# A two-layer scan kernel: the first layer's sums, gates and closings in a new order and in own PSUM banks, and backward steps of the second layer moved by a round

## The reference, cut to what matters

```python
# layer 0, per image, T = 3136 tokens, C = 192
k, v, r = xs @ Wk.T, xs @ Wv.T, xs @ Wr.T
x_bi = 0.5 * (wkv_scan(k, v) + flip(wkv_scan(flip(k), flip(v))))
h    = sigmoid(r) * x_bi
h    = layernorm(h) * ln_g + ln_b
x    = x + h @ Wo.T
# layer 1, per image: two selective scans (16 states, 384 inner channels)
x1, x2 = _layernorm(tok, g1, b1), _layernorm(tok, g2, b2)
x, z = x1 @ W_in_x.T, x2 @ W_in_z.T
y_f  = _branch(x, ...)              # conv of 4 taps, silu, dt, B, C, scan
y_b  = flip(_branch(flip(x), ...))
out  = ((y_f + y_b) * silu(z)) @ W_out.T + b_out
```

## Time and profile before

| | us |
|---|---|
| median of 3 runs | 21059.9 (21033.74 to 21079.35) |
| the profiled execution | 21187.9 |
| its span, first to last instruction | 21186.1 |
| TensorE / VectorE / GpSimd / ScalarE busy | 87% / 83% / 84% / 66% |
| mean granted TensorE clock | 0.912 of 2.4 GHz |

### The profile page before, as it was taken

The page is one execution under the profiler, slowest core; times in us unless marked ns, Lnnn a source line. Parts: engine busy times, 40 slices in busy tenths (PEclk is TensorE's granted clock), DMA queues, the critical chain, the costliest instruction groups (busy, mean ns, idle before and its releaser), DMA issues. The chain is left out here.

```text
span 21186.1 us, 179805 instructions
## 1 busy us (share of the span) xinstructions
PE 18392.8 (87%) x43392; PEld 7798.8 (37%) x43392; DVE 17639.1 (83%) x13967; ACT 14035.8 (66%) x35077; POOL 17697.7 (84%) x10548
## 2 busy tenths in 40 slices
PE   8888888888888888888888888888888888888888
PEld 3333433334333333333333333333333333333333
DVE  7878978889788897878978888787987879878788
ACT  5756757567576775757757577675766757667576
POOL 6978969789697896978969799796987969879699
PEclk8989989899899998989989999998998989989899
DMA  2313313233132331313313133231331313313133
GB/s 74 133 63 123 130 58 132 70 123 129 57 130 74 123 130 67 132 61 123 130 65 133 64 130 121 75 131 66 129 113 72 132 64 132 113 72 128 61 137 115
DMA packets 528855, 2178.88 MB, mean 103 GB/s; under 512 B 96328, under 2 KB 243424, under 8 KB 527648
## 3 DMA queue, kind: packets, MB, share of 16 engines
q1 hardware_dynamic: 527648, 2165.99, 28.3%
HBM read 1905.47 MB, written 245.63 MB: 102 GB/s over the span
## 5 line engine op out<-in xcount | busy, mean ns | idle before, releaser
L969 DVE TENSOR_TENSOR_SCAN arena<-ps,arena 128x897 f32<-128x897 f32 x5376 | 10979.3, 2063 | 762.7 <-ACT arena L1125 688.2
L1177 POOL TENSOR_TENSOR arena<-arena 128x896 f32<-128x896 f32 x5376 | 9985.8, 1873 | 904.4 <-DVE arena L969 560.9
L899 PE MATMUL ps<-arena,ident 128*128 128x448 f32 x21504 | 9168.2, 563 | 1134.1 <-POOL arena L1177 1128.8
L1109 ACT ACTIVATE ps<-arena,A 128x448 f32<-128x448 f32 x10752 | 6403.8, 630 | 2089.7 <-DVE arena L969 2055.6
L899 PEld LDWEIGHTS ps<-arena,ident 128*128 128x128 f32 x21504 | 4070.1, 196 | 5966.4 <-issue 3525.2
L1169 POOL TENSOR_TENSOR arena<-arena 128x896 f32<-128x896 f32 x2240 | 4675.3, 2087 | 0.0
L958 DVE TENSOR_TENSOR arena<-ps,arena 128x896 f32<-128x896 f32 x3136 | 3336.3, 1064 | 30.4 <-ACT ps L1071 30.4
L856 PE MATMUL ps<-arena,diag 128*128 128x448 f32 x5376 | 2181.3, 550 | 117.4 <-issue 115.6
L856 PEld LDWEIGHTS ps<-arena,diag 128*128 128x128 f32 x5376 | 1021.8, 192 | 1185.5 <-issue 1093.8
L1158 POOL TENSOR_TENSOR arena<-arena 128x448 f32<-128x448 f32 x672 | 763.2, 1137 | 455.3 <-DVE arena L938 455.3
L1125 ACT ACTIVATE arena<-arena 128x2 f32<-128x2 f32 x5376 | 1033.1, 192 | 53.3 <-DVE arena L969 53.3
(11 more groups left out here) (164 smaller groups left out, 20641.1 us busy)
## 6 DMA issues: line engine op xcount, KB each, us to landing
arena<-bc_rows SPq DMA_DIRECT2D x1792, 896.0 KB, 4.8
x_projected<-arena SPq DMA_DIRECT2D x112, 672.0 KB, 3.5
y_forward<-arena SPq DMA_DIRECT2D x112, 672.0 KB, 3.7
arena<-x_projected SPq DMA_DIRECT2D x112, 672.0 KB, 7.6
arena<-y_forward SPq DMA_DIRECT2D x112, 672.0 KB, 4.1
x<-in_x SPq DMA_DIRECT2D x119, 336.0 KB, 3.7
x_normed<-arena SPq DMA_DIRECT2D x112, 336.0 KB, 2.8
arena<-x_normed SPq DMA_DIRECT2D x112, 336.0 KB, 4.3
```

Source lines behind the costliest of these rows:

```text
L899: m = e.matmul(y, ident[:, :], pr[:, q % NPR, a * T:a * T + T], start=False, stop=p == NP - 1 and a == 1)
L969: e.tensor_tensor_scan(rev(hh[:, q % NH, 0:W2], s), rev(decays(q)[:, 0:W2], s), rev(bb[:, q % NB, 0:W2], s), car[:, k, n:n + 1] if i % NC ...
L1109: e.activation(two(decays(q))[:, a, :], dt[:, r % NDT, :], ACT.Exp, scale=Am[s][:, k, 2 * p + a:2 * p + a + 1]).then_inc(c_ex, 1)
L1177: e.tensor_tensor(pr[:, q % NPR, :].rearrange("p (a b) -> p a b", a=2), two(hh[:, q % NH, :]), cr[:, 2 * p:2 * p + 2, :], ALU.mult).then_i ...
```

## The change

Two lists of due rounds are changed, and with the first also who does what and in which bank.

First layer:
- The direction sum and the gate are issued tile by tile, an addition and its multiplication together (`HPOOL` and `HDVE`), on GpSimd over rounds 13.6 to 24.6. The tiles t = 0 and t = 1 of the last step (s = 6) go to VectorE (4 operations).
- GpSimd makes `ys` of unit U-3 in round U instead of U-4, behind `tn` instead of ahead of it.
- `BANKS` gives each closing two banks, one for k = 0 (and the sums) and one for k = 1. They are banks that the products, the keys and the recurrences have left by then.
- `mn` is split into `mA` (over the first 128 channels) and `mM` (the other 64). Two closings of one step are issued together: both `mA`, both `mM`, both first halves of `vr`, and so on.
- `rounds` gives every step of the closings its round. Closing 0 starts at 14.4 instead of 17.0, closings 1 and 2 at 18.6 instead of 20, 3 and 4 at 21.2 instead of 23, 5 and 6 at 23.5 instead of 26.

Second layer, all of it but one number on the backward side: `ye` one round later, the gate of tile 0 one round later, all `z1` to `z4` and `g` 0.3 to 0.4 rounds later, `p1` and the step sizes of tiles 0 and 1 by 0.6 to 0.7 rounds, the first convolution by 0.3. The forward side's `p1` goes from 0.9 to 1.2, in the same whole round.

```diff
-    def project(i, t, u):
+    def project(i, t, u, v):
         pe.append((t, "xp", i, 0))
-        act.append((t + 0.9, "p1", i, 0))
+        act.append((t + v, "p1", i, 0))
         sp.append((t + 1.5, "cw", i, 0))
...
-        act.extend([(t + 1.6, "z1", i, e), (t + 2.4, "z2", i, e), (t + 3, "z3", i, e), (t + 3.7, "z4", i, e)])
-        pool.append((t + 4.5, "g", i, e))
+        act.extend([(t + 2, "z1", i, e), (t + 2.7, "z2", i, e), (t + 3.3, "z3", i, e), (t + 4, "z4", i, e)])
+        pool.append((t + 4.8, "g", i, e))
...
-            for e, v in enumerate((1, 8.7, 10.7)):
+            for e, v in enumerate((1.3, 8.7, 10.7)):
                 conv(i, e, t + v)
-            project(i, t + 15.6, (1.2, 1.7, 5))
-            gate(i, 0, t + 20.6)
+            project(i, t + 15.6, (1.9, 2.3, 5), 1.5)
+            gate(i, 0, t + 21.6)
             gate(i, 1, t + 24)
...
-                dve.append((t + 0.5, "ye", i, e))
+                dve.append((t + 1.5, "ye", i, e))
...
+    BANKS = {MID: (JB, JB), MID + 1: (JB, (2, 3)), MID + 2: ((KB, VB), (2, 3)), MID + 3: ((0, 1), JB)}
+
+    def bank(n, k):
+        return ps[:, BANKS[CLOSE[n][0]][k][n % 2], 0:T]
+
+
+    HPOOL = [(MID, 0), (MID, 2), (MID + 1, 0), (MID + 1, 1), (MID + 1, 2), (MID + 2, 0), (MID + 2, 1), (MID + 2, 2),
+             (MID + 3, 2)]
+    HDVE = [(MID + 3, 0), (MID + 3, 1)]
+
...
+    def both_ways(s, t):
+
+        c = NC - 1 - s
+        n = 0 if s == MID else 2 + 3 * (s - MID - 1)
+        if t == 0:
+            return ys[:, 3 * s, :], rev(ys[:, 3 * c + 1, :], 1), n, 3 * s + 1 + (s == MID)
+        if t == 1:
+            return ys[:, 3 * c, :], rev(ys[:, 3 * s + 1, :], 1), n + 1, 3 * s + 2
+        return ys[:, 3 * s + 2, :], rev(sw[:, c, :], 1), n + (1 if s == MID else 2), 3 * s + 3
...
+        for s, t in HPOOL:
+            pool.append((3 * s + 3.6 + (t or s == MID) + (t == 2) * (s > MID), "h", s, t))
+        for s, t in HDVE:
+            dve.append((23.2 + 0.01 * t, "h", s, t))
+        rounds = {
...
+            MID + 2: dict(mA=21.2, mM=21.3, hc=23.3, sq=23.4, vr=23.8, rs=24.3, hn=24.2, o0=24.4, o1=24.6, x0=24.4, x1=24.6),
...
+            if n % 2 or not n:
+                pe += [(r["mA"], "mA", n, 0), (r["mM"], "mM", n, 0), (r["vr"], "vr", n, 0), (r["o0"], "o", n, 0),
+                       (r["o1"], "o", n, 1)]
+            dve += [(r["hc"], "hc", n, 0), (r["hn"], "hn", n, 0), (r["x0"], "xo", n, 0), (r["x1"], "xo", n, 1)]
+            act += [(r["sq"], "sq", n, 0), (r["rs"], "rs", n, 0)]
...
+                if name == "h":
+                    i = HDVE.index((n, k))
+                    a, b, m, units = both_ways(n, k)
+                    w.wait_ge(b_y, units)
+                    w.wait_ge(b_rg, m + 1)
+                    e.tensor_tensor(a, a, b, ALU.add).then_inc(b_hx, 1)
+                    w.wait_ge(b_hx, i + 1)
+                    e.tensor_tensor(a, a, sg[:, m, :], ALU.mult).then_inc(b_hv, 1)
+                    continue
...
+                if name == "mA":
                     w.wait_ge(b_rg, len(GATES))
-                    w.wait_ge(b_h, 3 * (s - MID) + 3)
-                    if n > 1:
-                        w.wait_ge(b_xo, nth(n - 2, 1) + 1)
-                    e.matmul(o, ones[:, :], ha, start=True, stop=False)
-                    e.matmul(o, ones[rows, :], hm, start=False, stop=True).then_inc(b_mn, 1)
+                    if s < MID + 3:
+                        w.wait_ge(b_h, HPOOL.index((s, 1 if s > MID else 0)) + 1)
+                    if s == MID + 1:
+                        w.wait_ge(b_xo, nth(0, 1) + 1)
+                    if s == MID + 2:
+                        w.wait_ge(b_kv, NU)
+                        w.wait_ge(b_bv, NU)
+                    if s == MID + 3:
+                        w.wait_ge(b_hv, len(HDVE))
+                        w.wait_ge(b_dn, NU)
+                    for m in two:
+                        e.matmul(bank(m, 0), ones[:, :], ys[:, 3 * CLOSE[m][1], :], start=True, stop=False)
+                if name == "mM":
+                    gated(w, s)
+                    for m in two:
+                        rows, f = late(m)
+                        e.matmul(bank(m, 0), ones[rows, :], rev(ys[rows, 3 * s + 2, :], f), start=False,
+                                 stop=True).then_inc(b_mn, 1)
...
+                        if k and s == MID + 1:
+                            w.wait_ge(b_dn, NU - 1)
+                        elif k:
+                            w.wait_ge(b_xo, nth(*{MID: (0, 0), MID + 2: (m - 2, 1), MID + 3: (m - 4, 0)}[s]) + 1)
...
-            u = U - 4
-            if 0 <= u < NU:
-                w.wait_ge(b_nw, u + 1)
-                e.tensor_tensor(ys[:, u, :], dn[:, u % 3, T:2 * T], tn[:, u % 2, :], ALU.mult).then_inc(b_y, 1)
+            u = U - 3
+            if 0 <= u < NU:
+                w.wait_ge(b_nw, u + 1)
+                e.tensor_tensor(ys[:, u, :], dn[:, u % 3, T:2 * T], tn[:, u % 2, :], ALU.mult).then_inc(b_y, 1)
```

88 lines of the change are left out of this document (42 added, 46 removed).

## The result

The changed kernel takes **20562.1 us** (20554.2 to 20586.7, 4 runs) against 21069.0 us (21033.7 to 21079.4) for the kernel before: a ratio of **0.976, 95% interval 0.975 to 0.978**, 507 us less. The direction was right and the time lies in the range of 20,400 to 20,960, but 158 us under the 20,720 that I named. The parts show why: one came out as worked out, one brought four times its term, one cost eight times what it was to bring.

The account below looks back on a forecast made before the run. GpSimd, fullest engine, was taken to limit the second layer, with waits around `ye`, and TensorE the first layer's tail. Gains 240 + 112 + 16 = 368 us; 21,060 - 368 + 28 = 20,720 us, range 20,400 to 20,960.

Parts of the forecast that it names:

- Part 1: Second layer, `ye` and backward steps a round later: VectorE scans during its wait, -15 us an item, -240 us in all.
- (b): Second layer, backward side: GpSimd comes to its floor, -4.7 us a chunk, run at 20,470 us; chance 0.12.
- (c): Second layer gains nothing, as TensorE or ScalarE becomes what the scan waits for: 20,960 us; chance 0.15.
- (d): Second layer slower, TensorE's next tile waiting for the later `ye`: +286 us, run at 21,250 or 21,380 us; chance 0.06.
- I give them no sum of their own: Second layer: moves other than `ye` only let the scan follow at once, with no separate gain counted.
- Part 2: First layer's tail behind the last recurrence: fewer matmuls left there, -7 us an item as the mean, -112 us.
- the gap of 4 us: First layer's tail at the upper clock: TensorE waits 4 us ahead of `mM` of closings 5 and 6.
- (e): First layer's tail: banks and pairs do nothing, TensorE being busy anyway; counted in the sum already, no chance given.
- a tail once low stays low: First layer's tail: once at the lower TensorE clock it remains there; used against the 20,400 us rival.
- (a): First layer's tail: clock stays up in nearly all items, 435 us gained instead of 112, run at 20,400; chance 0.14.
- Part 3: First layer, rounds 14 to 20 ahead of the last recurrence's end: about -1 us an item, -16 us.
- the term -4.0: First layer, rounds 14 to 20: VectorE's 4.0 us wait for the edge copy behind GpSimd's block of six goes.

Follow-up runs that it names:

- -17.3 alone: The kernel before with only the second layer's part of the change: 20908.4 us, ratio 0.987; its second layer is 17.3 us an item shorter.
- all alternated: The changed kernel with each closing's 128-partition and 64-partition matmuls issued one behind the other again, not paired: 21168.4 us, ratio to before 1.003.

## Why the prediction was right, and where not

**Part 1** held in mechanism and size. -15 us an item were said and -17.6 measured (-17.3 alone); five backward chunks 367 us, measured 365.78; the wait at `ye` below 300 us, measured 148.5; GpSimd at 355, measured 355.47. The idle time of five backward chunks came down to that of the forward side (10.3 against 12.7 us), which was the row I took the size from. Rivals (b), (c) and (d) fall: GpSimd kept 10.3 of its 23.4 us of idle time, now for TensorE, and TensorE waits at the skip matmul 7.9 us in five chunks (3.6 before), 0.5 at each of 15 places. Wrong in it was "I give them no sum of their own": the other moves are worth 3.0 us on top of `ye`.

**Part 2** was mis-sized: -7 us an item said, -28.2 measured. The chain worked out was close: `nw` at S + 10.5 (measured S + 10.0), the gap of 4 us up to S + 14 (3.18 us, up to S + 14.3). The pause of 3.65 us across S, ahead of `mM` of closings 3 and 4, was not in it. Two steps failed. First, the price of 1.74 to 1.79 us for every one of the 40 matmuls: the diff pairs the 64-partition matmuls of two closings, and I counted each of them at the price of one. The Trainium skill (TensorE: Matmul & The Clock Gate, section "Part 3: Packing small matmuls — row/col tiling") says that small matmuls on different tiles of the array run concurrently; the trace after agrees, with 1.87 us for two at the lower clock and 1.02 at the upper. The Trainium skill (TensorEngine Tiling (Array Packing), section "Gotcha 1: PSUM Pressure") wants a bank for each; here each has its own, and the shared one was not tried. Rival (e), that the banks and pairs do nothing because TensorE is busy in 30.00 of 30 us, was wrong for that reason: a busy engine says nothing about how much of it works. Second, "a tail once low stays low": true of the order of before (68.2 us all alternated), not of the new one. The estimate above puts 15.9 us on the first of these steps and 16.6 on the second, before the pauses take 11.1 back. Rival (a) had the outcome, at a chance of 0.14, by reasons that the runs don't bear out as they stood. That the pairs leave "no wait between sums" is not it: there are waits, and the tail of before had none in its 30 us. Nor is it activity alone, since TensorE was busy 30.00 of 30 us at 0.50 before and all alternated.

**Part 3** had the wrong sign: -1 us an item (-4 to +6) said, +8.3 to S measured, of which +7.6 behind round 14. S stands 160.5 us behind the table load, outside the 148 to 158 that I gave. The +2.4 us of work was right (2.2 measured). The step that failed is the term -4.0, "the new list breaks that block up": it does, and VectorE's wait behind it went from 3.7 to 1.2 us an item. But I put the new waits at nothing. I did not follow the chain of each early closing through the queues, where it puts 3 to 4 us ahead of the scan twice an item, 6.4 us in all, and smaller ones beside it: the idle time grows by 5.5 us where the sum had it fall by 4.0. All alternated, the rounds behind 14 are 17.6 us longer than before; the pairs take back 10.

**The sum.** 281 + 28.2 x 16 = 451, less 8.3 x 16 = 133, is 599 us for the profiled executions, against 601 measured and 368 said. Part 2 brought 339 us more than its term and part 3 cost 149 us more; that the time still lies in the range is in part luck, since the two misses point opposite ways. The timed runs give 507: the profiled execution of before was 119 us above the median of its runs, that of the changed kernel 25. I put this down to the number of tails at the upper clock, 32 us each. The changed kernel has no tail that stays at 0.50, and its runs lie within 33 us, where those of before reach over 286 us in one later comparison (20929.1 to 21214.8). The mean granted clock of those two runs is 0.926 and 0.910. Nine tails of 75.5 us at 0.50 instead of 43.7 us at 1.00 would make 286 us and, by estimate, 0.016 of mean clock, which is what these two differ by; the clock of the timed runs isn't recorded by item.

## What to carry to other kernels

Where a matmul uses half of the partitions, look for a partner on the other half and put the two behind each other, each with a bank of its own as here: it halves their time, and here the order also decided which clock the stretch ran at. Before costing a reordered queue by counts, ask which instructions become neighbours. And a chain over several engines that is issued early into queues of a full loop holds up the loop: move its head, and leave each step a round for its answer.
